# Mixture-of-experts tiles in the order of the routing batches, with the final sum and norm of finished batches placed inside the tile loop

## The chip, the cores and the metric

The program runs on one core of a Trainium2 chip. The metric is device time in microseconds (us) of one execution. Times below are medians of several executions, or rows of one profiled execution. The engines are TensorE (PE), VectorE (DVE), ScalarE (ACT), GpSimd (POOL) and SyncE (SP), which here only issues DMA transfers.

## The reference

16 sequences of 256 tokens, 256 channels, float32. A causal self-attention and a cross-attention (16 heads of 16 channels), each with a residual and a layer norm, give 4096 rows `x2`. They are followed by a mixture of 8 experts, of which every row takes 2:

```
logits = x2 @ router_w.T
topk_logits, topk_idx = top_k(logits, 2)
probs = softmax(topk_logits)
hmid = gelu(x2 @ w1[e].T + b1[e])        # 256 -> 512
y    = hmid @ w2[e].T + b2[e]            # 512 -> 256
out  = layernorm(x2 + sum over the 2 experts of prob * y)
```

## The kernel before

**Routing.** The attention part works through 32 blocks. In the second half of them each sequence's 256 rows are finished and routed in nine batches (`BATCHES`: seven of 4 x 128 tokens, two of 2 x 128). For each of its two experts a row gets the next free place in that expert's region of `xs_dram`, and POOL scatters the row there with its id and its two weights. `carry` holds, per expert, the next free place. After the last batch DVE turns the counts into a table (`tbli`, `aside`; L1428 to L1465): for each of 71 tiles of 128 gathered rows its expert and the place where it starts. Tiles stand by expert, all tiles of expert 0 first. Tiles past the last one are filled with rows that nobody reads.

**The tile loop** (`for j in range(TILES)`, 71 tiles). SP loads the tile's rows (`rows`, L477, 5 buffers) and the first-layer weights of its expert two tiles further on (`load_first(j + 2)`, L464, 512 KB, 4 buffers). Before it issues the weights of a tile it waits for `h_pe`, the first layer of the tile four places earlier. PE transposes the rows (L813), does the first layer (L824), transposes the next tile's rows, and then does the second layer of the tile before (L835). DVE adds the first bias (`add_first_bias`, L1473), ACT transposes out (L1034) and does the gelu (L1041), DVE adds the second bias, weighs, adds the residual and computes the row ids (`finish_tile`, L1483 to L1489), and POOL scatters the result into `p_dram` (L1636, 3 buffers `stored`). Each engine has one queue of instructions in program order, and SP's are in the order of its loop.

**The end.** When all 71 tiles are stored, SP loads the two halves of every token's sum from `p_dram` in six groups (`NORM_GROUPS`, L487), DVE adds them and takes mean and variance (`measure`, L1508 to L1517), ACT and DVE make the inverse root (L1055, L1057, L1525 to L1534), ACT normalises (L1063), and SP stores the rows (L492).

Of the kernel before, what the change touches and what calls it, by code (L numbers as in the profile page):

```python
# [10 lines left out]
I32 = mybir.dt.int32  # L11
# [27 lines left out]
NORM_GROUPS = (4, 4, 8, 8, 4, 4)  # L39
# [18 lines left out]
ROUTED = NT * max(BATCHES.values())  # L58

# [65 lines left out]
def decoder_block(nc, x, xT, ctxT, wqk_self, wv_self, wo_self, wq_x, wk_x, wv_x, wo_x, bo_self, bo_x,  # L125
# [4 lines left out]
    with ExitStack() as ctx:  # L130
# [82 lines left out]
        carry = sb("carry", [P, NE])  # L213
# [8 lines left out]
        cnt = sb("cnt", [P, 8, NE])  # L222
        cnti = sb("cnti", [P, 2, NE], I32)
        tbl = sb("tbl", [P, 2, TILES])
        tbli = sb("tbli", [P, 2, TILES], I32)
        aside = sb("aside", [P, TILES])
        surplus = sb("surplus", [P, TILES])
        jrows = sb("jrows", [P, TILES])
# [14 lines left out]
        def halves(group):  # L243

            n = NORM_GROUPS[group]
            at = sum(NORM_GROUPS[:group])
            flat = big[:] if at < 16 else w2s[:].rearrange("p c e f -> p (c e f)")
            k0 = (at % 16) * TOPK * E
            assert at % 16 + n <= 16
            return flat[:, k0:k0 + TOPK * n * E].rearrange("p (k n e) -> p k n e", k=TOPK, n=n)  # L250


# [47 lines left out]
        table_link, table_ready = sem("table_link"), sem("table_ready")  # L300
        pads_out = sem("pads_out")
# [17 lines left out]
        jrow = small[:, 32:32 + TILES]  # L319
        tri8 = small[:, 128:192].rearrange("p (e f) -> p e f", e=NE)  # L320
        assert 32 + TILES <= 128
# [50 lines left out]
        def stored_in(o):  # L372

            return len(range(o, TILES, OUT_BUFFERS))

        def expert_of(eng, j):
            return eng.value_load(tbli[0:1, 0, j:j + 1], min_val=0, max_val=NE - 1)

# [7 lines left out]
        def _(sp):  # L386
# [85 lines left out]

            for j in range(TILES):
                start = sp.value_load(tbli[0:1, 1, j:j + 1], min_val=0, max_val=PADS + NE * P - P)
                if j >= ROW_BUFFERS:
                    sp.wait_ge(rowid_ready, j - ROW_BUFFERS + 1)
                sp.dma_start(rows[:, j % ROW_BUFFERS, :], xs_dram[bass.ds(start, P), :]  # L477
                             ).then_inc(rows_in[j % ROW_BUFFERS], 16)
                load_first(j + 2)

            for o in range(OUT_BUFFERS):
                sp.wait_ge(stored[o], 16 * stored_in(o))
            for group, n in enumerate(NORM_GROUPS):
                r0 = P * sum(NORM_GROUPS[:group])
                src = p_dram[0:TOPK * N, :].rearrange("(k n) e -> k n e", k=TOPK)[:, r0:r0 + n * P, :]
                for k in range(TOPK):
                    sp.dma_start(halves(group)[:, k], src[k].rearrange("(p n) e -> p n e", p=P)  # L487
                                 ).then_inc(halves_in[group], 16)
            for group, n in enumerate(NORM_GROUPS):
                r0 = P * sum(NORM_GROUPS[:group])  # L490
                sp.wait_ge(normed, group + 1)
                sp.dma_start(out[r0:r0 + n * P, :].rearrange("(p n) e -> p n e", p=P), halves(group)[:, 1]  # L492
                             ).then_inc(out_done, 16)
            sp.wait_ge(out_done, 16 * len(NORM_GROUPS))

        @block.tensor
        def _(pe):
# [301 lines left out]

            pe.wait_ge(table_ready, 2)  # L800
# [48 lines left out]
        def _(act):  # L849
# [192 lines left out]

            turn_out(0)
            for j in range(TILES):
                if j + 1 < TILES:
                    turn_out(j + 1)
                gelu(j)

            def seed_group(group):
                if group >= len(NORM_GROUPS):  # L1050
                    return
                n = NORM_GROUPS[group]
                act.wait_ge(moments_ready, group + 1)
                yy, t0 = ls[:, group % 2, 1, 0:n], ls[:, group % 2, 2, 0:n]
                act.activation(t0, moments[:, group % 2, 0:n, 1], ACT.Ln, bias=eps[:, 1:2]).then_inc(tail_log, 1)  # L1055
                act.wait_ge(tail_log, group + 1)
                act.activation(yy, t0, ACT.Exp, scale=-0.5).then_inc(tail_seeded, 1)  # L1057

            def normalise_group(group):
                act.wait_ge(norm_ready, group + 1)  # L1060
                d = halves(group)
                for i in range(NORM_GROUPS[group]):
                    ins = act.activation(d[:, 1, i], d[:, 0, i], ACT.Identity, bias=ls[:, group % 2, 4, i:i + 1],  # L1063
                                         scale=ls[:, group % 2, 1, i:i + 1])
                ins.then_inc(normed, 1)

            act.preload_act_table_set("natural_log_exp_and_others")
            seed_group(0)
            for group in range(len(NORM_GROUPS)):
                seed_group(group + 1)  # L1070
                normalise_group(group)

        @block.vector
        def _(dve):
# [32 lines left out]
            def prepare_tables():  # L1107
                dve.tensor_scalar(rev[:], iota8, -1.0, float(NE), ALU.mult, ALU.add)
                dve.tensor_copy(carry[:], iota8_region)
                dve.tensor_scalar(jrows[:], jrow, float(P), None, ALU.mult)  # L1110
                dve.tensor_scalar(surplus[:], jrow, float(P), float(P * (1 - TOPK * N // P)), ALU.mult, ALU.add)
                dve.tensor_scalar(tokid[:], jrow[:, 0:N // P], float(P), pcol, ALU.mult, ALU.add
# [242 lines left out]
            def take_ranks(n):  # L1355
                if n is None:
# [4 lines left out]
                o = ring_slot(job).rearrange("p (j e) -> p j e", e=NE)  # L1361
                dve.tensor_tensor(rank[:, 0:nt, :], o[:, 0:nt, :],
                                  carry[:].unsqueeze(1).to_broadcast([P, nt, NE]), ALU.add).then_inc(router_link, 1)
                dve.wait_ge(router_link, next(n_route))
                dve.tensor_tensor(carry[:], o[:, nt, :], carry[:], ALU.add).then_inc(drained_by(job), 1)
# [16 lines left out]
            for q in range(QUARTERS):  # L1382
# [45 lines left out]
            dve.tensor_tensor(cnt[:, 1], carry[:], iota8_region, ALU.subtract).then_inc(table_link, 1)  # L1428
            dve.wait_ge(table_link, next(n_table))
            dve.tensor_scalar(cnti[:, 1], cnt[:, 1], float(P - 1), None, ALU.add).then_inc(table_link, 1)  # L1430
            dve.wait_ge(table_link, next(n_table))
            dve.tensor_scalar(cnti[:, 1], cnti[:, 1], 7, None, ALU.logical_shift_right
                              ).then_inc(table_link, 1)
            dve.wait_ge(table_link, next(n_table))
            dve.tensor_copy(cnt[:, 2], cnti[:, 1]).then_inc(table_link, 1)
            dve.wait_ge(table_link, next(n_table))
            w88 = sq[:].rearrange("p t e -> p (t e)")[:, 0:NE * NE].rearrange("p (a b) -> p a b", a=NE)
            dve.tensor_tensor(w88, tri8, cnt[:, 2].unsqueeze(1).to_broadcast([P, NE, NE]), ALU.mult
                              ).then_inc(table_link, 1)
            dve.wait_ge(table_link, next(n_table))  # L1440
            dve.tensor_reduce(cnt[:, 3], w88, AX.X, ALU.add).then_inc(table_link, 1)
            dve.wait_ge(table_link, next(n_table))
            dve.tensor_scalar(cnt[:, 4], cnt[:, 2], -float(P), float(REGION), ALU.mult, ALU.add
                              ).then_inc(table_link, 1)
            wj = [a.rearrange("p t e -> p (t e)")[:, 0:TILES * NE].rearrange("p (j e) -> p j e", e=NE)
                  for a in (sq[:], qkn[:, 0])]

            def every_j(ap):
                return ap.unsqueeze(1).to_broadcast([P, TILES, NE])

# [262 lines left out]
```

## Time and profile before

| | |
|---|---|
| median of 3 runs | 1171.24 us (1169.45 to 1173.36) |
| time of the profiled execution | 1169.33 us |
| its span, first to last instruction | 1167.6 us |
| PE busy | 1029.7 us, 88% |
| DVE busy | 724.1 us, 62% |
| ACT busy | 596.7 us, 51% |
| POOL busy | 267.0 us, 23% |
| mean DMA rate | 119 GB/s over the span |

The busy share is an average over three stages. The attention part runs to about 804 us, the routing of the last rows and the table to 850 us, the tile loop to 1120 us, and the end to 1167.6 us. In the tile loop PE is busy nearly all the time, in the end not at all. What a change is worth is read from the stage in which it lies.

### The profile page before, as it was taken

How to read it: one execution, taken by the hardware profiler on the slowest of the kernel's cores; microseconds unless marked ns; L12 is line 12 of the kernel's file. 1: busy time of each engine (PE TensorE's matmuls, PEld its weight loads, DVE VectorE, ACT ScalarE, POOL GpSimd, SP SyncE). 2: the span in 40 equal slices, each digit the busy share in tenths (PEclk: the TensorE clock that was granted, in tenths of full speed). 3: DMA queues.
4: the chain of work that ended last, by engine and by line, in shares of the span. 5: the costliest groups of instructions: out<-in, count | busy, mean ns of one | idle time of the engine just before them, and what ended most of it. 6: DMA issues, size and time to landing. Idle time of an engine off the chain costs nothing.

```text
span 1167.6 us, 29067 instructions
## 1 busy us (share of the span) xinstructions
PE 1029.7 (88%) x10925; PEld 767.3 (66%) x10925; DVE 724.1 (62%) x1584; ACT 596.7 (51%) x1024; POOL 267.0 (23%) x309
## 2 busy tenths in 40 slices
PE   6899999999999999999999999877189999999930
PEld 3556666666666666666666666545179999999930
DVE  4656666666677877677878787753524444444446
ACT  3567767767755566665555655654122222222225
POOL 1053232232232200000212121132512222222210
PEclk9999999999999999999999999998589999999975
DMA  7117446446441000100101100011267777677656
GB/s 290 29 36 249 149 144 209 147 146 211 142 126 30 12 20 12 47 12 20 40 26 35 34 26 30 13 40 40 92 203 215 219 215 210 213 214 218 202 201 253
DMA packets 95078, 139.25 MB, mean 119 GB/s; under 512 B 11264, under 2 KB 68992, under 8 KB 93920
## 3 DMA queue, kind: packets, MB, share of 16 engines
q1 hardware_dynamic: 88320, 114.98, 31.6%
q0 software_dynamic: 6624, 22.42, 4.9%
q8 instruction: 91, 1.49, 0.5%
q14 instruction: 43, 0.35, 0.1%
HBM read 76.56 MB, written 60.29 MB: 117 GB/s over the span
## 4 chain that ended last, share of the span: by engine, by line
PE 80%; issue 6%; DVE 5%; ACT 3%; DMA 2%; SPq 2%; another core or an unknown queue 0%; ACTq 0%; DVEq 0%; POOLq 0%
PE PS L824 11%; PE PS L561 11%; PE PS L835 11%; PE PS L582 10%; PE PS L531 5%; PE PS L635 5%; PE PS L639 5%; PE PS L706 5%; PE PS L653 4%; PE PS L680 3%; PE PS L538 2%; PE PS L669 2%; PE PS L534 2%; ACT pT L904 2%; PE PS L813 1%
## 5 line engine op out<-in xcount | busy, mean ns | idle before, releaser
L1158 DVE TENSOR_REDUCE part<-PS 128x6 f32<-128x768 f32 (+1 forms) x256 | 270.1, 1087 | 117.9 <-PE PS L538 85.0
L904 ACT ACTIVATE pT<-PS 128x768 f32<-128x768 f32 (+1 forms) x256 | 220.8, 915 | 102.6 <-PE PS L561 89.8
L561 PE MATMUL PS<-big 32*128 32x256 f32 (+1 forms) x2048 | 133.2, 373 | 20.4 <-issue 11.7
L1595 POOL TENSOR_SCALAR_AFFINE_SELECT pT<-pT 128x512 f32<-128x512 f32 x128 | 84.2, 659 | 278.7 <-ACT pT L904 274.9
L824 PEld LDWEIGHTS PS<-oT,big 128*128 128x128 f32 x1136 | 139.8, 194 | 5.4 <-ACT oT L1034 1.8
L824 PE MATMUL PS<-oT,big 128*128 128x128 f32 x1136 | 140.6, 278 | 1.0 <-ACT oT L1034 1.0
L561 PEld LDWEIGHTS PS<-big 32*128 32x128 f32 x2048 | 95.9, 184 | 62.5 <-issue 61.2
L582 PE MATMUL PS<-pT,vaug 128*32 128x256 f32 (+1 forms) x2048 | 125.0, 361 | 13.6 <-DVE sq L1227 3.5
L835 PE MATMUL PS<-w2s,qkn 128*128 x568 | 134.5, 380 | 0.0
L1034 ACT ACTIVATE oT<-PS 128x256 f32<-128x256 f32 x71 | 27.2, 383 | 192.7 <-PE PS L813 192.7
L1615 POOL DMA_INDIRECT xs_dram<-rows_all,posi x64 | 62.1, 971 | 250.1 <-PE PS L531 174.2
L1636 POOL DMA_INDIRECT p_dram<-pT,rowid x71 | 68.4, 964 | 212.6 <-DVE rowid L1489 208.4
L835 PEld LDWEIGHTS PS<-w2s,qkn 128*128 128x128 f32 x568 | 102.4, 190 | 11.5 <-issue 0.5
L915 ACT ACTIVATE oT<-PS 128x256 f32<-128x256 f32 x128 | 49.0, 383 | 113.5 <-PE PS L582 111.6
L582 PEld LDWEIGHTS PS<-pT,vaug 128*32 128x32 f32 x2048 | 58.8, 109 | 64.7 <-issue 39.5
L1473 DVE TENSOR_TENSOR qkn<-PS,b1T 128x512 f32<-128x512 f32 x71 | 49.1, 692 | 61.0 <-PE PS L824 61.0
L1483 DVE TENSOR_TENSOR pT<-PS,w_self 128x256 f32<-128x256 f32 x71 | 30.2, 425 | 88.5 <-PE PS L835 88.5
L531 PE MATMUL PS<-big 32*128 32x256 f32 x1024 | 74.2, 404 | 7.0 <-ACT pT L904 6.8
L639 PE MATMUL PS<-w_self,xin 128*128 128x512 f32 x128 | 66.9, 649 | 1.3 <-DVE w_self L1085 1.3
L531 PEld LDWEIGHTS PS<-big 32*128 32x128 f32 x1024 | 47.4, 186 | 20.8 <-issue 18.9
L1041 ACT ACTIVATE qkn<-qkn 128x512 f32<-128x512 f32 x71 | 44.7, 630 | 19.8 <-DVE qkn L1473 18.9
L1268 DVE TENSOR_TENSOR y<-PS,xb 128x512 f32<-128x512 f32 x32 | 22.1, 692 | 40.9 <-PE PS L706 37.3
(170 smaller groups left out, 1533.8 us busy)
## 6 DMA issues: line engine op xcount, KB each, us to landing
big<-w SPq DMA_DIRECT2D x71, 512.0 KB
xs_dram<-zrow SPq DMA_DIRECT2D x24, 1496.0 KB, 9.8
oT<-xs_dram SPq DMA_DIRECT2D x71, 136.0 KB
xin<-xT SPq DMA_DIRECT2D x16, 256.0 KB, 2.9
w2s<-w POOLq DMA_DIRECT2D x1, 4096.0 KB, 15.8
xb<-x SPq DMA_DIRECT2D x16, 256.0 KB, 11.2
xin<-ctxT SPq DMA_DIRECT2D x16, 256.0 KB, 2.8
big<-nmaxT SPq DMA_DIRECT2D x128, 4.0 KB
```

Of the source, the lines that this page charges most:

```text
L531: ins = pe.matmul(o, q, a[r0:r1, 1, g, :], start=True, stop=True)
L561: ins = pe.matmul(o, keys, a[r0:r1, 0, g, q0:T], start=True, stop=True)
L582: ins = pe.matmul(o[PADDED * i:PADDED * (i + 1), q0:T], vaug[:, n % 4, kt, head(g, i), :], pT[:, k % 2, i, kt * T:kt * T + T - q0], start= ...
L635: ins = pe.matmul(o[:, e0:e0 + E], a1[:, c, t * P:(t + 1) * P], w[:, c, :], start=(c == 0), stop=(c == KC - 1))
L639: ins = pe.matmul(o, a[:, c, t * P:(t + 1) * P], w_qk[:, c, :], start=(c == 0), stop=(c == KC - 1))
L824: ins = pe.matmul(moe_bank(1, j % 2)[:, f * P:(f + 1) * P], w1s[:, j % W1_BUFFERS, c, f * P:(f + 1) * P], xsT[:, j % 2, c * P:(c + 1) * P] ...
L835: ins = pe.matmul(moe_bank(3, j % 2)[:, 0:E], hact[:, j % 2, c * P:(c + 1) * P], w, start=(c == 0), stop=(c == FC - 1))
L904: act.activation(pT[:, k % 2, 2 * half:2 * half + 2, 0:wide], src, ACT.Exp).then_inc((exp_a, exp_b)[half], 1)
L1158: dve.tensor_reduce(dst, src, AX.X, ALU.max, negate=True).then_inc((max_a, max_b)[half], 1)
L1595: pool.affine_select(d, d, [[0, 2], [0, 2], [1, P]], ALU.is_ge, 0.0, base=0, channel_multiplier=-1).then_inc(masked, 1)
L1615: pool.indirect_dma_start(out=xs_dram, out_offset=bass.IndirectOffsetOnAxis(ap=posi[:, batch_index(last), c:c + 1], axis=0), in_=rows_all[ ...
L1636: pool.indirect_dma_start(out=p_dram, out_offset=bass.IndirectOffsetOnAxis(ap=rowid[:, o, 0:1], axis=0), in_=ye[:, o], in_offset=None).the ...
```

## The change

1. The routing counts are kept after each batch (`carries`, 10 rows instead of one `carry`), and the table orders tiles by the batch in which they begin, and by expert within a batch. After `DONE_BY[g]` tiles every row of the batches up to g has been computed: 15, 23, 31, 39, 47, 55, 63, 67 and 71 tiles.
2. The table is worked out on the partitions, one tile in each, turned by three PE transposes, and copied out of PSUM.
3. The final groups are the nine batches: seven of 4 x 128 tokens, two of 2 x 128. For a group g SP loads the halves in its loop step `DONE_BY[g] + 6`, DVE adds a quarter of them in each of its steps `DONE_BY[g] + 4` to `+ 7` and measures them, DVE works the roots out in steps `+ 8` to `+ 11` (by shift and subtraction and three Newton steps, without ACT), ACT normalises in steps `+ 13` and `+ 14`, and SP stores in its step `+ 21`. Groups 6, 7 and 8 (`ENDING`) take their roots after the loop in the old way.
4. The loaded halves lie in `big` behind the weight buffers, in `vaug` and in `rows_all`.

```diff
+NORM_GROUPS = tuple(NT * k for _, k in sorted(BATCHES.items()))
+DONE_BY = tuple((TOPK * P * sum(NORM_GROUPS[:g + 1]) - P) // P + NE for g in range(CLASSES))
+FETCH, MEASURE, ROOTS, NORMALISE, SEND = 6, 4, 8, 13, 21
+ENDING = tuple(g for g in range(CLASSES) if DONE_BY[g] + ROOTS + 4 > TILES)
...
+        def group_step(j, at):
+            for g in range(CLASSES):
+                if g not in ENDING[1:] and 0 <= j - DONE_BY[g] - at < 4:
+                    return g, j - DONE_BY[g] - at
+            return None
...
+            def fetch_group(group):
+                for o in range(OUT_BUFFERS):
+                    sp.wait_ge(stored[o], 16 * stored_by(DONE_BY[group], o))
+                n, r0 = NORM_GROUPS[group], P * sum(NORM_GROUPS[:group])
+                src = p_dram[0:TOPK * N, :].rearrange("(k n) e -> k n e", k=TOPK)[:, r0:r0 + n * P, :]
+                for k in range(TOPK):
+                    sp.dma_start(halves(group)[:, k], src[k].rearrange("(p n) e -> p n e", p=P)
+                                 ).then_inc(halves_in[group], 16)
...
                 load_first(j + 2)
-
-            for o in range(OUT_BUFFERS):
-                sp.wait_ge(stored[o], 16 * stored_in(o))
-            for group, n in enumerate(NORM_GROUPS):
...
+                if j - FETCH in DONE_BY:
+                    fetch_group(DONE_BY.index(j - FETCH))
+                if j - SEND in DONE_BY:
+                    send_group(DONE_BY.index(j - SEND))
+
+            for group in range(CLASSES):
+                if DONE_BY[group] + FETCH < TILES:
+                    continue
+                if group == CLASSES - 1:
+                    send_group(ENDING[0] - 1)
+                fetch_group(group)
+            for group in ENDING:
+                send_group(group)
...
                 gelu(j)
+                place = group_step(j, NORMALISE)
+                if place is not None and place[1] < 2:
+                    group, step = place
+                    act.wait_ge(norm_ready, group + 1)
+                    for i in range(2):
+                        normalise_rows(group, 2 * step + i)
...
+            def add_halves(group, i):
+                if i == 0:
+                    dve.wait_ge(halves_in[group], 32)
+                d = halves(group)
+                dve.tensor_tensor(d[:, 0, i], d[:, 0, i], d[:, 1, i], ALU.add).then_inc(added, 1)
...
             for j in range(1, TILES):
                 before, e = e, expert_of(dve, j)
                 add_first_bias(j, e)
+                add_halves_at(j)
                 finish_tile(j - 1, before)
+                measure_at(j)
             finish_tile(TILES - 1, e)
```

SP's queue in the tile loop, one step of it before: `tbli` is read for the tile's place, the rows are loaded, `tbli` is read for the expert, and the weights (`big<-w`) go out behind the wait for `h_pe`.

```order
L474 TENSOR_LOAD tbli
L474 ISA x2
L477 ISA [waits rowid_ready]
L477 DMA oT<-xs_dram 128x272
L461 TENSOR_LOAD tbli
L461 ISA x2
L464 ISA [waits h_pe]
L464 DMA big<-w 128x2x512
```

The same step of the changed kernel where a group is fetched (group 3, whose halves lie in `vaug`):

```order
L523 ISA [waits rowid_ready]
L523 DMA oT<-xs_dram 128x272
L492 TENSOR_LOAD tbli
L492 ISA x2
L495 ISA [waits h_pe]
L495 DMA big<-w 128x2x512
L510 DMA vaug<-p_dram 128x1024 [waits stored_2,stored_1,stored_0]
L510 DMA vaug<-p_dram 128x1024
```

The two loads of 512 KB stand behind the weight load of the same step, and so behind its wait for `h_pe`.

DVE's queue in the tile loop, one tile before: first bias of tile j, then the finishing of tile j - 1.

```order
L377 TENSOR_LOAD tbli
L377 ISA x2
L1473 ISA [waits hact_ready,h_pe]
L1473 TENSOR_TENSOR qkn<-PS,b1T 128x512
L1483 ISA [waits stored_0,y_pe]
L1483 TENSOR_TENSOR pT<-PS,w_self 128x256
L1487 ISA [waits biased]
L1487 SCALAR_TENSOR_TENSOR pT<-pT,oT 128x256
L1489 ISA
L1489 TENSOR_TENSOR rowid<-oT,aside 128x1
```

The same of the changed kernel in the first of a group's measuring steps (group 0, j = 19), up to the next tile's first bias:

```order
L1544 ISA [waits hact_ready,h_pe]
L1544 TENSOR_TENSOR qkn<-PS,b1T 128x512
L1569 TENSOR_TENSOR big<-big 128x256 [waits halves_in_0]
L1554 ISA [waits stored_0,y_pe]
L1554 TENSOR_TENSOR pT<-PS,w_self 128x256
L1558 ISA [waits biased]
L1558 SCALAR_TENSOR_TENSOR pT<-pT,oT 128x256
L1560 ISA
L1560 TENSOR_TENSOR rowid<-oT,aside 128x1
L1573 BN_STATS stats<-big 128x6 [waits added]
L397 TENSOR_LOAD tbli
L397 ISA x2
```

A sum of halves that waits for `halves_in_0` now stands between the first bias of tile j and the finishing of tile j - 1, and a statistics instruction before the next tile's expert is read.

## Rows read from the trace of the kernel before

**Rows 1.** Windows, tile loop: us, busy per engine, PEclk, DMA share, GB/s
```profile
850.00:1100.00 250.00, 248.67 (x1715) 234.27 (x1716) 108.66 (x259) 68.50 (x134) 61.69 (x64) 0.99 0.70 212
```

**Rows 2.** Chain that ended last, one tile: start us, us, what
```profile
1082.75 0.22 PE PS L813 x2
1082.97 1.73 PE PS L835 x8
1084.70 1.78 PE PS L824 x16
```

**Rows 3.** Timeline, one tile: start us, us, engine, line, tiles [idle before]
```profile
1053.04 0.69 DVE L1473 TENSOR_TENSOR qkn<-PS,b1T 128x512 f32<-128x512 f32 x1 [0.66 <-PE PS L824]
1053.07 0.56 SPq L464 DMA_DIRECT2D big<-w  x1
...
1053.77 0.63 ACT L1041 ACTIVATE qkn<-qkn 128x512 f32<-128x512 f32 x1 [0.23 <-DVE qkn L1473]
...
1054.99 0.42 DVE L1483 TENSOR_TENSOR pT<-PS,w_self 128x256 f32<-128x256 f32 x1 [1.26 <-PE PS L835]
...
1055.96 0.15 DVE L1489 TENSOR_TENSOR rowid<-oT,aside 128x1 int32<-128x1 f32 x1
```

**Rows 4.** Timeline, start of the tile loop, weight loads and first bias
```profile
843.50 2.06 SPq L464 DMA_DIRECT2D big<-w  x2
...
847.53 0.55 SPq L464 DMA_DIRECT2D big<-w  x1
...
850.00 0.56 SPq L464 DMA_DIRECT2D big<-w  x1
...
855.48 0.55 SPq L464 DMA_DIRECT2D big<-w  x1
855.52 0.69 DVE L1473 TENSOR_TENSOR qkn<-PS,b1T 128x512 f32<-128x512 f32 x1 [13.12 <-PE PS L824]
```

**Rows 5.** Timeline, the end: last second layer to last norm
```profile
1117.68 2.28 PE L835 MATMUL PS<-w2s,qkn 128*128 x9
...
1124.49 3.18 SPq L487 DMA_DIRECT2D big<-p_dram  x6
...
1129.34 1.22 DVE L1508 TENSOR_TENSOR big<-big 128x1024 f32<-128x1024 f32 x1 [8.10 <-DMA big<-p_dram]
...
1132.04 0.38 DVE L1517 BATCH_NORM_AGGREGATE moments<-stats 128x2 f32<-128x6 f32 x4
...
1159.11 0.38 DVE L1517 BATCH_NORM_AGGREGATE moments<-stats 128x2 f32<-128x6 f32 x4 [1.60 <-ACT w2s L1063]
...
1160.16 4.04 ACT L1063 ACTIVATE w2s<-w2s,ls 128x256 f32<-128x256 f32 x8
...
1160.67 0.16 DVE L1534 SCALAR_TENSOR_TENSOR ls<-moments,ls 128x4 f32<-128x4 f32 x1
```

**Rows 6.** DMA issues, 1124.3 to 1124.8 us: count, KB each, us to landing
```profile
big<-p_dram SPq DMA_DIRECT2D x1, 512.0 KB, 3.6
```

**Rows 7.** Timeline of DVE and PE around the table
```profile
836.24 0.16 DVE L1428 TENSOR_TENSOR cnt<-carry,small 128x8 f32<-128x8 f32 x1
...
839.11 0.74 DVE L1453 TENSOR_TENSOR sq<-cnt,small 128x568 f32<-128x568 f32 x1
...
842.17 0.23 DVE L1465 TENSOR_TENSOR tbli<-tbl,jrows 128x71 int32<-128x71 f32 x1
...
850.32 0.66 PE L813 MATMUL PS<-ident,oT 128*128 128x128 f32 x2 [18.14 <-DMA oT<-xs_dram]
```

**Rows 8.** Timeline of PE, two places with an idle gap
```profile
737.42 2.06 PE L531 MATMUL PS<-big 32*128 32x256 f32 x16 [2.29 <-ACT pT L904]
739.41 1.79 PE L582 MATMUL PS<-pT,vaug 128*32 128x256 f32 x16
...
804.39 1.07 PE L582 MATMUL PS<-pT,vaug 128*32 128x256 f32 x16 [1.79 <-ACT pT L904]
```

**Rows 9.** Windows behind those gaps; columns as in Rows 1
```profile
737.00:741.00 4.00, 3.58 (x32) 1.96 (x32) 2.63 (x6) 1.68 (x3) 0.59 (x1) 0.57 0.02 4
805.00:809.00 4.00, 3.88 (x27) 2.82 (x16) 0.86 (x3) 0.77 (x3) 3.08 (x4) 0.60 0.35 125
```

More of the change, by code:

```diff
@@ L245, in halves @@
             n = NORM_GROUPS[group]
[L246 to L249, printed above, removed]
+            if group < 2:
+                flat, first = big[:, W1_BUFFERS * KC * F:], 0
+            elif group < 4:
+                flat, first = vaug[:].rearrange("p n t h d -> p (n t h d)"), 2
+            else:
+                flat, first = rows_all[:].rearrange("p t e -> p (t e)"), 4
+            k0 = TOPK * E * sum(NORM_GROUPS[first:group])
             return flat[:, k0:k0 + TOPK * n * E].rearrange("p (k n e) -> p k n e", k=TOPK, n=n)
+        wide = pflat[:, 0:3 * P].rearrange("p (a t) -> p a t", a=3)
         cst = pflat[:, 0:3 * P].rearrange("p (a t) -> p a t", a=3)
@@ L318, in decoder_block @@
         idcol = small[:, 17:18]
[L319 removed]
+        jrow = small[:, 32:32 + N // P]
         tri8 = small[:, 128:192].rearrange("p (e f) -> p e f", e=NE)
[L321 removed]
         def bc(ap, n):
@@ L479, in _ @@
                 load_first(j + 2)
-            for o in range(OUT_BUFFERS):
-                sp.wait_ge(stored[o], 16 * stored_in(o))
-            for group, n in enumerate(NORM_GROUPS):
[L484 to L494, printed above, removed]
+                if j - FETCH in DONE_BY:
[10 more added lines that the diff above has]
+                send_group(group)
+            sp.wait_ge(out_done, 16 * CLASSES)
         @block.tensor
@@ L798, in _ @@
                     fold_bias()
+            pe.wait_ge(columns_ready, 3)
+            for i in range(3):
+                ins = pe.transpose(bank(0)[:, i * P:(i + 1) * P], wide[:, i, :], ident[:])
+            ins.then_inc(table_pe, 1)
             pe.wait_ge(table_ready, 2)
@@ L1434, in _ @@
[L1434 to L1449, printed above, removed]
-            dve.tensor_tensor(wj[0], every_j(cnt[:, 3]), bc(jrow, NE), ALU.is_le).then_inc(table_link, 1)
@@ new lines, in _ @@
+            linked(dve.tensor_tensor(grown[:], grown[:], ends[:], ALU.subtract))
+            dve.tensor_scalar(offset[:, CLASSES * NE:], ends[:, CLASSES - 1, NE - 1:NE], -float(P), float(PADS),
+                              ALU.mult, ALU.add)
+            linked(dve.tensor_tensor(grown[:], grown[:], begun[:, 0:CLASSES], ALU.add))
+            linked(dve.scalar_tensor_tensor(out=o8, in0=grown[:], scalar=float(P), in1=of_batches(iota8_region),
+                                            op0=ALU.mult, op1=ALU.add))
@@ new lines, in sum_up @@
+            def sum_up(group):
+                n = NORM_GROUPS[group]
+                for i in range(n):
+                    dve.wait_ge(norm_link, next(n_norm))
+                if group >= 2:
+                    dve.wait_ge(normed, group - 1)
+                for i in range(n):
+                    ins = dve.bn_aggr(moments[:, group % 2, i, :], stats[:, 4 * (group % 2) + i, :])
+                if group in ENDING:
+                    ins.then_inc(moments_ready, 1)
+                else:
+                    ins.then_inc(norm_link, 1)
+                    dve.wait_ge(norm_link, next(n_norm))
```

203 lines of the change are left out of this document (132 added, 71 removed).

## The prediction

> **What bounds the kernel now.** I read the page first: PE is busy 88% of the span, so the question is where the other 12% lie. The windows by stage answer it. In the tile loop PE is busy 248.67 of 250 us, DVE 108.66, ACT 68.50, and the DMA engines 70% at 212 GB/s [rows 1]: PE is the bound, and everything else is cover. The chain that ended last shows what one tile costs there: 0.22 us of transposes, 1.73 of the second layer, 1.78 of the first, in all 3.73 us, with nothing in between [rows 2]. In the end stage PE does nothing. It stops at 1117.68 + 2.28 = 1119.96, call it E, and the span ends at 1167.6. So 47.6 us of the program lie behind E, with loads, sums and norms in a chain [rows 5]. This is what the change can win. What it can lose lies in the two other places it touches: the table before the loop, where PE waits, and the loop, where any microsecond in which PE stands still is lost whole.
>
> **The end stage, cost by cost.** Now: the last tile is stored and the first load of halves is issued 4.5 us behind E (1124.49). Then come 4096 tokens, until the last norm at 1160.16 + 4.04 = 1164.20, and 3.4 us more to the end for the last store [rows 5]. After: the same 4.5 us stand, since the last group must wait for the last tile. The last group has 256 tokens: two loads of 256 KB. One of 512 KB landed in 3.6 us [rows 6], and I add 0.4 for the second issue: they are there at E + 8.5. For four rows of tokens per partition DVE took from 1129.34 to 1132.04 + 0.38 = 1132.42, 3.1 us; two rows take half, and links a little: 1.7, E + 10.2. From the end of the last aggregate (1159.49) to the end of its last root step (1160.83) are 1.35 us. Two rows of norm at 4.04 / 8 = 0.505 are 1.0. With 3.4 for the last store the end is at E + 16.0. Groups 6 and 7 lie under the wait for the last tile: they are three times the work of group 8, some 5 us of DVE and 3 of ACT by the same rates, and start at E or before. The end stage falls from 47.6 to 16.0: **31.6 us won**. Bounds: 29, if groups 6 and 7 reach into group 8, and 33.
>
> **The table.** Now 14 DVE instructions run from 836.24 to 842.40, 6.2 us, four of them of 0.74 us [rows 7]. The other ten so take 0.32 each with their gaps. After: 23 instructions before the transposes, two of the big kind: 21 x 0.32 + 2 x 0.74 = 8.2. Then three PE transposes of 128x128, of which two took 0.66 there (PE's clock is low in that stage) [rows 7]: 1.0. Three copies out of PSUM, less than the 0.42 of one twice as wide [rows 3]: 0.9 in all. Two hops between engines: 0.3. Together 10.4, so **4.2 us lost**. Nothing covers it: SP's first weight load goes out behind the table, at 843.50 [rows 4]. Bounds: 2.5 (small instructions at 0.22) and 5.5.
>
> **The loop: DVE's and ACT's added work is covered.** A tile in which DVE sums and measures a quarter of a group adds 1.22 / 4 = 0.3 and about 0.35 us. A root step adds three or four linked operations of 0.16 to 0.2, the first of them four aggregates (0.38) as well [rows 5]: 0.6 to 1.1. DVE finishes a tile at 1055.96 + 0.15, 3.1 us behind its start at 1053.04 [rows 3]. It then comes up to 1.3 us late to the next bias. That bias and the gelu take 1.36 us (1053.04 to 1054.40), and PE wants them only 0.22 + 3.73 = 3.95 us behind the first layer. So 2.6 us are spare: nothing lost. Two norms on ACT, 1.0 us in two tiles of a group, go the same way.
>
> **The loop: DVE's wait for the halves is not covered.** Here I followed who waits for whom. At the start of the loop SP issues two weight loads, then two more, and the fifth at 855.48, beside the first bias of the first tile at 855.52 [rows 4]. The same pair stands in each tile, 1053.07 and 1053.04 [rows 3]. So SP's load of weights i + 4 goes out when the first layer of tile i ends, in SP's loop step i + 2. The change fetches a group in SP's step `DONE_BY + 6`, behind that load. This is the end of the first layer of tile `DONE_BY + 4`. And `DONE_BY + 4` is the tile behind whose bias DVE waits for the same halves. Both are released by one event, T. DVE must therefore wait out the whole landing, and the finishing of a tile, the reading of an expert and the next bias are queued behind it.
>
> How long: the fetch is issued at about T + 0.8, behind 0.56 us of weight issue. Two loads of 512 KB took 1129.34 - 1124.49 = 4.85 us with no traffic before them [rows 5], which gives T + 5.7. The 512 KB of weights are ahead of them. At 212 / 0.70 = 303 GB/s [rows 1] these alone move for 1.7 us, in part while the fetch starts up. I take T + 7.0. With the tile's rows and its store ahead as well (776 KB, 2.6 us) it is T + 8.3. Behind the landing: sum 0.3, finishing 1.1 (1054.99 to 1056.11), statistics 0.35, the expert's number at most the 0.66 us that DVE idles now, I take 0.5, bias and gelu 1.36 [rows 3], hops 0.2: 3.8. PE gets tile i + 1 at T + 10.8. It wanted it at T + 0.22 + 2 x 3.73 = T + 7.7. **PE stands still for 3.1 us** (1.3 at the early landing with the shortest chain, 4.6 at the late one), in groups 0 to 5. For group 6 SP's last steps have no weights left to wait for, so its fetch goes out some 2 us before T, and 2.6 us of slack take the rest.
>
> The Trainium skill, "DMA: Bandwidth & Descriptors", section "Anatomy of one DMA", fits a load as 2.0 us plus bytes at 436 GB/s. For the two loads that is 4.4 us, where this trace has 4.85, and the measurement decides; the page speaks of loads issued by GpSimd. With the weights ahead it would be T + 5.7, a stall of 1.8 us and an estimated total of 1162 us.
>
> **The clock behind a gap.** In the trace PE's granted clock falls from its upper level (2.4 GHz) to the lower (1.2) behind short gaps too. Behind a gap of 2.29 us the next four microseconds have a mean of 0.57, and behind one of 1.79 us 0.60 [rows 8, 9]. In the first case L582 takes 1.79 us, and 1.07 where the clock is high. Over that and L531 (2.06, by the same ratio 1.23) the loss is 0.72 + 0.83 = 1.5 us [rows 8]. The tile loop's matmuls are denser than those, so that a gap may be borne better there. Ends: nothing, and 3.0 for two such stretches. I take 1.5.
>
> **The sum.** Six groups at 3.1 + 1.5 = 4.6 are 27.6 us lost. 1169.33 - 31.6 + 4.2 + 27.6 = 1169.5 for an execution like the profiled one. This lies 1.9 us below the median of 1171.24, so the median to expect is between 1169.5 and 1171.4: **1171 us**. Two large terms cancel; the point where the loop's loss eats the gain is (31.6 - 4.2) / 6 = 4.57 us per group.
>
> **Rivals.**
> - *The wait is there, but PE keeps its upper clock.* For it speaks the dense loop, against it [rows 9]. 1169.33 - 31.6 + 4.2 + 6 x 3.1 = **1160.5**. Chance 0.17.
> - *The halves land early,* at T + 5.7: a stall of about 1.8 us, and 1.5 for the clock: 6 x 3.3 = 19.8, **1161.7**. For it speaks that a single load landed in 3.6 us and the second only 1.3 us later [rows 5, 6], so these move faster than the weights; against it, that the weights are issued first on the same queue. Chance 0.12. The fit of the Trainium skill named above would give this one.
> - *The kernel becomes slower: the landing is late.* With send, weights, rows and store ahead the halves land at T + 8.3 or later, PE stands still for 4.6 us, and the gap is long enough that the clock stays low for two stretches: 7.6 x 6 = 45.6, **1187.5**. It decides from 4.57 us per group. For it speaks that in four of six groups a store of 512 KB goes out one step before the fetch; against it, that this store has a whole tile to drain. Chance 0.15.
> - *There is no wait worth the name,* because SP runs further ahead than [rows 4] say. Then only the end and the table count: **1142**. The two rows beside each other speak against it. Chance 0.06.
>
> **How the numbers follow.** My own case has a chance of 0.50 and a range of 1163 to 1180. 0.3% (3.5 us) is about what a measurement of this kernel can tell from no change. Within my case I give 0.16 below 1167.7, 0.20 between, 0.14 above 1174.8. Faster: 0.16 + 0.17 + 0.12 + 0.06 = 0.51. Same: 0.20. Slower: 0.14 + 0.15 = 0.29. The range of 1153 to 1185 leaves out the case without a wait and the later half of the slower one.
>
> **What would show it.** In the profile after: DVE's sum of halves with six waits of about 6 us for the load, each followed by an idle gap of PE of some 3 us before a second layer and a window of clock 0.5; a distance from PE's last matmul to the span's end of 16 us; a first transpose of the tile loop about 4 us later than 850.32; all other tiles at 3.73 us. Wrong would make it: waits of DVE shorter than 3.5 us, a gap without a fall of the clock, or tiles that take longer than 3.73 us where no group is fetched.

## The result and the profile after

The changed kernel takes **1187.97 us** (median of 4 runs, 1186.28 to 1190.98), the kernel before beside it 1170.37 (4 runs, 1169.45 to 1173.36). The ratio is 1.0149, 95% interval 1.0119 to 1.0178: 17.6 us slower. I had forecast 1171, so almost no change, with a range of 1153 to 1185, a chance of 0.51 for faster and of 0.29 for slower. The time is outside the range, and on the side that I held less likely than faster.

The profiled execution took 1189.02 us. The page's first lines, to be held against a span of 1167.6 us and a PE that was busy 88% of it:

```profile
span 1187.3 us, 29198 instructions
...
PE 1051.2 (89%) x10928; PEld 780.8 (66%) x10928; DVE 735.8 (62%) x1687; ACT 594.2 (50%) x1018; POOL 267.7 (23%) x309
```

PE issues the same matmuls, but for the three transposes of the table (10928 against 10925), and is busy for 21.5 us more. That alone doesn't tell whether it works or works slowly. The windows do. First the whole tile loop, from the first transpose to PE's last matmul, then two stretches of it (us, busy time of PE, PEld, DVE, ACT, POOL, granted clock, DMA share, GB/s):

```profile
857.85:1172.78 314.93, 285.96 (x1846) 263.36 (x1846) 148.66 (x439) 85.47 (x168) 66.78 (x69) 0.94 0.63 210
...
947.00:949.00 2.00, 2.00 (x11) 2.00 (x11) 1.32 (x4) 0.00 (x0) 0.00 (x0) 0.50 0.30 109
...
1090.00:1092.00 2.00, 0.00 (x0) 0.00 (x0) 1.86 (x6) 0.66 (x2) 0.97 (x1) 0.50 0.25 66
```

The same window of the kernel before, for the same stretch of its program:

```profile
850.32:1119.96 269.64, 268.63 (x1846) 252.36 (x1846) 117.77 (x281) 74.46 (x144) 66.50 (x69) 0.99 0.68 204
```

The loop is 45.3 us longer with the same 1846 records of PE. Of these, 28.0 are idle time of PE (314.93 - 285.96, less the 1.0 of before), and 285.96 - 268.63 = 17.3 are longer busy time. Most of that is the clock: it has a mean of 0.94 in place of 0.99, and in the second row it is 0.50, the lower level of 1.2 GHz, while PE is busy all the time. Taken in windows of 1 us, busy time times the missing share of the clock adds up to 14.0 us in the seven places where the clock falls (an estimate from these windows). In the loop before, the clock is below its upper level only in the first 7 us. The other 3.3 us are at full clock. PE's records overlap where it runs without a break: transposes last 0.38 us and the next matmul begins 0.22 behind them. Beside a gap they stand alone and count whole; that this is the 3.3 us is an argument, but a run below has 3.3 us more busy time too, with gaps and no fall of the clock. The waits of the loop say for whom (us in total, times, longest):

```profile
DVE rows_all L1569 <- DMA rows_all<-p_dram: 21.0, 3, 8.9
PE PS L862 <- DMA oT<-xs_dram: 19.3, 9, 9.2
PE PS L884 <- DVE pT L1554: 17.0, 7, 2.6
DVE vaug L1569 <- DMA vaug<-p_dram: 14.1, 2, 7.1
DVE big L1569 <- DMA big<-p_dram: 13.2, 2, 7.2
```

Seven waits of DVE for halves, 48.3 us together; seven waits of PE for DVE's finishing of a tile, 17.0 us; and nine of PE for the rows of a tile, of which the longest, 9.2, is the first transpose's before the loop. The other eight hold 10.1 us. The timeline of group 0 shows how they hang together:

```profile
933.13 0.69 DVE L1544 TENSOR_TENSOR qkn<-PS,b1T 128x512 f32<-128x512 f32 x1 [0.66 <-PE PS L873]
933.16 0.56 SPq L495 DMA_DIRECT2D big<-w  x1
933.84 1.00 SPq L510 DMA_DIRECT2D big<-p_dram  x2
...
935.93 0.35 SPq L523 DMA_DIRECT2D oT<-xs_dram  x1
...
941.01 0.42 DVE L1569 TENSOR_TENSOR big<-big 128x256 f32<-128x256 f32 x1 [7.19 <-DMA big<-p_dram]
...
941.36 0.42 DVE L1554 TENSOR_TENSOR pT<-PS,w_self 128x256 f32<-128x256 f32 x1
941.36 0.44 PE L862 MATMUL PS<-ident,oT 128*128 128x128 f32 x2 [0.92 <-DMA oT<-xs_dram]
...
942.92 0.69 DVE L1544 TENSOR_TENSOR qkn<-PS,b1T 128x512 f32<-128x512 f32 x1
...
944.41 2.49 PE L884 MATMUL PS<-w2s,qkn 128*128 x8 [2.60 <-DVE pT L1554]
946.69 3.14 PE L873 MATMUL PS<-oT,big 128*128 128x128 f32 x16
```

Read it as a chain. DVE's bias and SP's weight load begin 0.03 us apart, so one event T (933.13) releases both. The fetch goes out at T + 0.71, and DVE stands at its sum until T + 7.88. The finishing, the next bias and the gelu follow, and PE gets its second layer at T + 11.28 after two gaps, 0.92 and 2.60 us. The eight matmuls of second layer then take 2.49 us and the sixteen of first layer 3.14, where the same rows of an undisturbed tile have 1.89 and 1.95 (936.77 and 934.77; the 1.73 and 1.78 of [rows 2] are from start to start): the price of the clock. The rows of a tile, issued behind the megabyte of halves on SP's queue (935.93), are the 0.92, and DVE's late finishing is the 2.60.

The end stage, which answers to [rows 5]:

```profile
1168.99 3.79 PE L884 MATMUL PS<-w2s,qkn 128*128 x16
...
1177.33 0.79 SPq L510 DMA_DIRECT2D rows_all<-p_dram  x2
...
1180.62 0.76 DVE L1569 TENSOR_TENSOR rows_all<-rows_all 128x256 f32<-128x256 f32 x2 [3.29 <-DMA rows_all<-p_dram]
...
1183.77 1.09 ACT L1094 ACTIVATE rows_all<-rows_all,ls 128x256 f32<-128x256 f32 x2 [0.82 <-DVE ls L1657]
```

PE ends at 1168.99 + 3.79 = 1172.78, and 14.5 us of program follow where there were 47.6.

The table, which answers to [rows 7]:

```profile
840.34 0.23 DVE L1497 TENSOR_TENSOR ends<-carries,small 128x72 f32<-128x72 f32 x1
...
847.72 0.90 PE L847 MATMUL PS<-ident,pT 128*128 128x128 f32 x3 [11.29 <-DVE pT L1529]
...
857.85 0.66 PE L862 MATMUL PS<-ident,oT 128*128 128x128 f32 x2 [9.23 <-DMA oT<-xs_dram]
```

From its first instruction to the first transpose of the loop it takes 17.5 us, before 14.1 (836.24 to 850.32). So the two profiles differ by -33.1 (end) + 3.4 (table) + 45.3 (loop) = 15.6 us, and the table begins 4.1 us later, which makes the 19.7 of the spans. Most of those 4.1 can't be laid to the change: 3.4 of them are already there where PE begins its first block (30.46 against 27.02), and in the runs below, whose code up to there is that of the change, this point lies anywhere between 26.7 and 30.5.

### The profile page after: what moved, and what is told of

Read it like the earlier page. It is cut to its first block and busy times, and to the rows that moved or that the text cites. A ratio compares the mean times of both kernels' runs of the same rounds, so it can differ in the third digit from the quotient of the medians.

```text
span 1187.3 us, 29198 instructions
## 1 busy us (share of the span) xinstructions
PE 1051.2 (89%) x10928; PEld 780.8 (66%) x10928; DVE 735.8 (62%) x1687; ACT 594.2 (50%) x1018; POOL 267.7 (23%) x309
## 5 line engine op out<-in xcount | busy, mean ns | idle before, releaser
L884 PE MATMUL PS<-w2s,qkn 128*128 x568 | 144.4, 400 | 17.9 <-DVE pT L1554 17.0
L873 PEld LDWEIGHTS PS<-oT,big 128*128 128x128 f32 x1136 | 145.0, 200 | 6.2 <-ACT oT L1083 1.8
L873 PE MATMUL PS<-oT,big 128*128 128x128 f32 x1136 | 144.7, 283 | 1.0 <-ACT oT L1083 1.0
L884 PEld LDWEIGHTS PS<-w2s,qkn 128*128 128x128 f32 x568 | 107.4, 199 | 33.3 <-issue 20.6
```

Of the source, the lines that this page charges most:

```text
L873: ins = pe.matmul(moe_bank(1, j % 2)[:, f * P:(f + 1) * P], w1s[:, j % W1_BUFFERS, c, f * P:(f + 1) * P], xsT[:, j % 2, c * P:(c + 1) * P] ...
L884: ins = pe.matmul(moe_bank(3, j % 2)[:, 0:E], hact[:, j % 2, c * P:(c + 1) * P], w, start=(c == 0), stop=(c == FC - 1))
```

## The experiments

All ratios below are against the kernel before, run on the same chip beside them. Apart from the change itself they come in three sets, each on a chip of its own: the table alone and the fetch at 4, 5 and 7; then the next four; then the last three. The kernel before had a median of 1171.4, 1171.89 and 1164.39 us in them, so ratios are compared and not times. The loop runs from the first transposes behind the table to PE's last matmul.

| kernel | median us | ratio (95%) | loop | of it PE busy | end |
|---|---|---|---|---|---|
| the change | 1187.97 | 1.0149 (1.0119, 1.0178) | 314.9 | 286.0 | 14.5 |
| table alone | 1176.07 | 1.0038 (1.0021, 1.0054) | 269.7 | 268.6 | 48.1 |
| fetch at 4 | 1159.87 | 0.9899 (0.9868, 0.9929) | 286.7 | 274.4 | 14.6 |
| fetch at 5 | 1182.8 | 1.0085 (1.0053, 1.0117) | 310.9 | 284.2 | 14.6 |
| fetch at 7 | 1204.24 | 1.0271 (1.0232, 1.0309) | 334.4 | 286.9 | 14.5 |
| DVE two tiles later | 1173.02 | 1.0010 (0.9993, 1.0027) | 297.5 | 279.7 | 14.7 |
| fetch ahead of weights | 1170.79 | 0.9992 (0.9966, 1.0019) | 297.6 | 280.4 | 14.6 |
| fetch in quarters | 1149.5 | 0.9817 (0.9785, 0.9848) | 276.6 | 272.0 | 14.6 |
| fetch on ACT's queue | 1152.15 | 0.9824 (0.9786, 0.9861) | 283.1 | 275.4 | 14.6 |
| fetch at 4, rows ahead | 1132.91 | 0.9720 (0.9693, 0.9747) | 270.0 | 268.9 | 14.5 |
| the change, rows ahead | 1178.59 | 1.0109 (1.0075, 1.0144) | 320.7 | 286.4 | 14.5 |
| quarters, rows ahead | 1130.32 | 0.9712 (0.9687, 0.9737) | 268.5 | 267.5 | 14.6 |

Loop, busy and end are of one profiled execution each.

### When the fetch goes out: step 4, 5 or 7

The theory said that only the place of the fetch in SP's loop makes DVE wait. One number changes:

```diff
-FETCH, MEASURE, ROOTS, NORMALISE, SEND = 6, 4, 8, 13, 21
+FETCH, MEASURE, ROOTS, NORMALISE, SEND = 4, 4, 8, 13, 21
```

and 5 or 7 in the two others.

> The change with one number different: a group's halves are fetched two loop steps of SP earlier (FETCH = 4 in place of 6), everything else as in the change. Theory (DVE waits for halves that are asked for by the same event that releases it): the halves lie there when DVE comes, no gap of PE, no fall of its clock, and the loop goes back from 315 us to about 270. About 1143 us, so some 45 below the change and 27 below before. Rival (the added DMA traffic or DVE's added work stretches the loop by itself): the loop stays above 300 us and the time above 1175.

> As the change, fetched one step later (FETCH = 7). Theory: each of the seven groups in the loop waits one tile period more, 7 x 3.73 = 26 us: 1210 to 1218 us. Rival (traffic or added work): no different from the change, 1188.

> As the change, fetched one step earlier (FETCH = 5). Theory: the landing moves 3.73 us towards DVE, from 7 to 9 us behind the event down to 3.4 to 5.2. PE had 3.9 us of slack less the chain of 3.4, so only the groups that land late keep a gap of under 1 us: 1143 to 1150 us. Rival (traffic or added work): above 1175, as with two steps.

At 7 the kernel is slower than before by 2.7%, and the seven gaps of PE before the second layer add up to 45.0 us, where the change has 17.0. The direction is the one that the wait gives, the size is smaller: 1204 and not 1210 to 1218, since DVE's waits grew by 2.3 us a group and not by a tile's 3.73 (64.7 in all, against 48.3). At 4 the kernel gets faster than before, though not the 1143 us of the theory: the loop is 28.2 us shorter than in the change, and no gap of PE is put down to DVE any more. So the wait of DVE is a cause. But at 4 some 17 us of the loop's loss stayed, and at 5 nearly all of it, although the DVE waits were down to 2.9 to 5.1 us. There PE's idle gaps add up to 25.7 us, and 23.9 of them stand before transposes. My expectation for 5 was wrong by over 30 us. The timeline of fetch at 5 shows what took the place of the wait:

```profile
994.57 1.81 SPq L510 DMA_DIRECT2D vaug<-p_dram  x2
996.43 0.42 SPq L516 DMA_DIRECT2D result<-big  x1
...
997.61 0.35 SPq L523 DMA_DIRECT2D oT<-xs_dram  x1
...
1005.91 0.69 PE L862 MATMUL PS<-ident,oT 128*128 128x128 f32 x2 [4.73 <-DMA oT<-xs_dram]
```

The rows of a tile (136 KB) are issued at 997.61 and PE gets them 8.3 us later: a megabyte of halves and 512 KB of output were issued on SP's queue just ahead. In this run the send of group g and the fetch of group g + 2 fall in one SP step (21 = 16 + 5). The five groups with both gave gaps of 3.8 to 5.0 us, and the two first, which have no send beside them, 0.4 and 1.6. So most of what the fetch at 5 costs goes with the burst of both together, and the step of the fetch changes two things: how early the halves are asked for, and how far they are from a send. No run moved the send alone. With the fetch at 4, where the send comes a step later, a gap before transposes that is put down to the rows is 1.20 us at most:

```profile
964.51 0.44 PE L862 MATMUL PS<-ident,oT 128*128 128x128 f32 x2 [1.20 <-DMA oT<-xs_dram]
```

Of its 11.4 us of added gaps the profile puts 4.0 down to the rows; 7.3 have no releaser (1.5 before the transposes of group 0, 5.8 before second layers). That these too hang on when the rows are issued is shown further down, where the rows go out earlier and all of these gaps go.

### The table by itself

The new table and its transposes, with the old loop and the old end stage.

> The new order of the tiles and the new table on DVE and PE, with the old tile loop and the old end stage (all 4096 tokens summed and normed after the last tile). Theory: costs only the longer table, 3 to 4 us: 1173 to 1175 us. Rival (the order of the tiles by batch makes the tile loop slower, or the start of the program is 3.4 us later because of the added setup): 1177 or more, the loop longer than 270 us or the first block later.

```profile
858.62:1128.27 269.65, 268.64 (x1846) 252.61 (x1846) 117.70 (x281) 74.45 (x144) 66.49 (x69) 0.99 0.66 204
```

The loop is 269.65 us long, before 269.64. The order of tiles costs nothing, the table 4.5 us (0.38%; 3 to 4 were expected, and 4.2 in the prediction).

### Halves as late as before, DVE two tiles later

This leaves the fetch where the change has it and takes the wait away from the other side:

```diff
-FETCH, MEASURE, ROOTS, NORMALISE, SEND = 6, 4, 8, 13, 21
+FETCH, MEASURE, ROOTS, NORMALISE, SEND = 6, 6, 10, 14, 22
...
-                if g not in ENDING[1:] and 0 <= j - DONE_BY[g] - at < 4:
+                if g not in ENDING and 0 <= j - DONE_BY[g] - at < 4:
...
-            sum_up(ENDING[0])
+            measure(ENDING[0])
```

> The fetch stays where the change has it (SP's step DONE_BY + 6), but DVE sums and measures two tiles later (MEASURE 6, ROOTS 10, NORMALISE 14, SEND 22; group 6 is measured behind the loop). First theory, of two costs of a fetch: DVE's wait for the halves is gone here, and what is left is that the tile's rows stand behind 1 MB on SP's queue: gaps of PE of 0.5 to 1.5 us before a transpose, loop 280 to 290 us, total 1157 to 1165 us, like the run with the fetch two steps earlier. Rival (DVE's wait is all there is): no gaps, about 1147 us. Rival (traffic itself slows the loop): above 1180.

There is no DVE wait for halves left in the loop. It is still 27.9 us longer than before, with 16.8 us of gaps, 14.8 of them before transposes:

```profile
1068.42 1.04 SPq L510 DMA_DIRECT2D rows_all<-p_dram  x2
1069.52 0.42 SPq L516 DMA_DIRECT2D result<-vaug  x1
...
1070.73 0.31 SPq L523 DMA_DIRECT2D oT<-xs_dram  x1
...
1079.33 0.69 PE L862 MATMUL PS<-ident,oT 128*128 128x128 f32 x2 [4.29 <-DMA oT<-xs_dram]
```

That is the second cost without the first, but not at the size that it has in the change: this edit moves the send into the fetch's step as well (22 = 16 + 6). The two groups without a send have gaps of 0.16 and 0.60 us, the next four with one 2.60 to 4.29 (the last, with a single tile left to load, 0.50), and with them 1173 us came out and not 1157 to 1165. The clock falls behind these gaps too: of the 11.1 us by which PE's busy time is longer, 9.1 are at the lower level (from the 1 us windows, as above).

### Fetch and send ahead of the weight load

If the weights ahead of the halves were what delays them, issuing the halves first should help.

```diff
+                if j - FETCH in DONE_BY:
+                    fetch_group(DONE_BY.index(j - FETCH))
+                if j - SEND in DONE_BY:
+                    send_group(DONE_BY.index(j - SEND))
                 load_first(j + 2)
-                if j - FETCH in DONE_BY:
-                    fetch_group(DONE_BY.index(j - FETCH))
-                if j - SEND in DONE_BY:
-                    send_group(DONE_BY.index(j - SEND))
```

(with `FETCH` at 4).

> As the run with FETCH = 4, but fetch and send are issued ahead of the step's weight load and not behind it, so about one microsecond or more earlier, and the next tile's rows have one megabyte less directly before them. If the remaining gaps of PE (0.3 to 1.5 us before a transpose, seven times) come from rows that queue behind the fetch: they shrink to under 0.5 us, total 1147 to 1155 us. Rival (the gaps come from the total traffic of the DMA engines in these tiles): unchanged, 1157 to 1163.

It moved the wrong way, against both expectations: slower than fetch at 4 by 0.9%. Group 1 of this run:

```profile
954.44 0.38 PE L862 MATMUL PS<-ident,oT 128*128 128x128 f32 x2
...
955.70 0.81 SPq L510 DMA_DIRECT2D big<-p_dram  x2
957.33 0.56 SPq L495 DMA_DIRECT2D big<-w  x1
958.67 0.36 SPq L523 DMA_DIRECT2D oT<-xs_dram  x1
...
964.27 0.44 PE L862 MATMUL PS<-ident,oT 128*128 128x128 f32 x2 [2.21 <-DMA oT<-xs_dram]
```

and of the run with the fetch at 4, up to the gap shown above (964.51):

```profile
955.68 0.38 PE L862 MATMUL PS<-ident,oT 128*128 128x128 f32 x2
...
956.02 0.56 SPq L495 DMA_DIRECT2D big<-w  x1
956.76 0.93 SPq L510 DMA_DIRECT2D big<-p_dram  x2
958.77 0.35 SPq L523 DMA_DIRECT2D oT<-xs_dram  x1
```

The same bytes stand ahead of the next rows in both, and the rows take the same time from issue to use, 5.6 and 5.7 us. But they are issued 4.2 us behind the transposes of the step here and 3.1 there: with the halves first, the weights go out 2.55 us later and the rows 1.1 us later. The gap is longer by 1.0 us. Over the loop seven such gaps of 1.2 to 2.6 us make 13.5. So putting the halves first makes what stands behind them late, and it is the next rows that PE misses.

### Smaller pieces, another queue, rows a step earlier

Three edits that take the rows out from behind the burst in different ways, all with the fetch at 4 or its like. In quarters, one for each of four SP steps:

```diff
+            def fetch_quarter(group, i):
...
+                    sp.dma_start(halves(group)[:, k, i], src[k].rearrange("(p n) e -> p n e", p=P)[:, i]
+                                 ).then_inc(quarter_in[i], 16)
```

(the store in quarters too). On ACT's queue, ACT issues both, the fetch at its iteration `DONE_BY + 2`:

```diff
+                        act.dma_start(halves(group)[:, k], src[k].rearrange("(p n) e -> p n e", p=P)
+                                      ).then_inc(halves_in[group], 16)
```

And SP issues each tile's rows one step earlier:

```diff
+            load_rows(0)
             for j in range(TILES):
+                load_rows(j + 1)
                 load_first(j + 2)
```

> The fetch of a group is cut in four pieces of 256 KB, one per loop step from DONE_BY + 4 on, each waited for by the sum of that quarter alone, and the send in four pieces of 128 KB from DONE_BY + 17 on. The same bytes, never more than 256 KB ahead of a tile's rows. Theory (rows behind a burst in SP's queue): no gaps, loop at 270 us, total 1143 to 1148 us. Rival (total traffic, or smaller descriptors of 1 KB, cost as much): 1157 or more.

> Whole groups again, but fetch and send are issued by ACT on its own queue, at the time at which the run with FETCH = 4 issues them on SP's. If it is the order within SP's queue that delays the rows: the two queues share the DMA engines packet by packet, the rows are delayed less, total 1145 to 1153 us. Rival (the DMA engines are simply busy with the megabyte): as with FETCH = 4, 1157 to 1163.

> FETCH = 4 with whole bursts of 1 MB on SP's queue, and every tile's rows loaded one loop step earlier than in the change (step j loads the rows of tile j + 1). Theory (rows lack the lead to stand behind a burst): the lead grows from 1.6 periods to 2.6, no gap before a transpose is left, total 1145 to 1150 us. Rival (the DMA engines cannot carry the bursts beside the tiles): 1157 or more, as with FETCH = 4 alone.

All three are faster than fetch at 4 (ratios 0.9817, 0.9824 and 0.9720 against 0.9899). The quarters leave 3.7 us of gaps, only 0.7 of it before a transpose, and are the run with 3.3 us more busy time and no fall of the clock behind the first 7 us. The run on ACT's queue came out as expected, the quarters 1.5 us above the expected 1143 to 1148, and the rows a step earlier below their 1145 to 1150, of which some 7 us are the faster set. Of the three, only the rows a step earlier bring the loop back whole. Quarters first, then rows ahead:

```profile
855.72:1132.34 276.62, 271.96 (x1846) 252.58 (x1846) 149.37 (x439) 86.17 (x168) 67.02 (x69) 0.99 0.79 239
...
848.25:1118.29 270.04, 268.94 (x1846) 252.62 (x1846) 149.03 (x439) 86.33 (x168) 66.80 (x69) 0.99 0.76 245
```

The loop with rows ahead is 0.4 us longer than before, with 245 GB/s in place of 204 and DVE busy for 149 us in place of 118. So neither DVE's and ACT's added work nor the added traffic costs PE anything, once nothing waits for a transfer that is issued too late. On ACT's queue some of the loss stays (6.7 us of added gaps, 2.9 of them put down to the rows, and two DVE waits of 1.1 and 1.0 us), so the order on one queue isn't all of it; that rows issued with little time to spare also share the DMA engines with the burst is a likely reading that no run isolates.

The rival to this reading was that the rows alone are what makes the change slow. The same edit, made to the change with its fetch at 6:

> The change itself (FETCH = 6) with the rows loaded one step earlier. Theory of two costs: the rows' part goes and DVE's wait stays: DVE waits 6 to 9 us in each group, PE has one gap of 2.5 to 3.5 us before a second layer and none before a transpose, the clock falls behind it, loop 300 to 308 us, total 1176 to 1182 us. Rival (the two overlap so far that only DVE's wait counts): 1188, unchanged.

```profile
932.63 0.42 DVE L1575 TENSOR_TENSOR big<-big 128x256 f32<-128x256 f32 x1 [7.95 <-DMA big<-p_dram]
...
936.03 2.50 PE L890 MATMUL PS<-w2s,qkn 128*128 x5 [4.50 <-DVE pT L1560]
```

No gap before a transpose is left, and the seven before the second layer have grown from 17.0 to 33.3 us: the loop is not shorter at all. The two costs lie over each other, since in each group the late rows only take up time that PE would have spent waiting for DVE. The ratio is 1.0109 against 1.0149, and their intervals overlap, so these runs don't tell the two kernels apart. The median of 1178.59 lies in the expected 1176 to 1182, but for the wrong reason: the kernel before was some 7 us faster in this set, while the expected loop of 300 to 308 us measured 320.7. (The profile shown is the slowest execution of this kernel, 1186.24 us, so its loop is longer than the usual.)

### Both together

Quarters, and the rows a step earlier.

> The fetch and the send in quarters, and the rows one step earlier. Both theories of the loop's cost say that nothing is left: loop 269.6 to 272 us, and with the table 2.5 longer and the end at 14.6 us a total of 1141 to 1146 us, the shortest of all. Rival (the gaps that the quarters left are those of the traffic): 1149 as before.

1130.32 us beside 1164.39 for the kernel before, 0.9712 (0.9687 to 0.9737): faster than both kernels, and below the expected 1141 to 1146 by more than the 7 us of this set. Behind the first two tiles, which wait for ACT for 0.5 us each as in every run, the profile lists no idle gap of PE in its loop, and the loop of 268.5 us is no longer than before. Against rows ahead by itself (0.9720) the intervals overlap, so the quarters add nothing that these runs can tell.

## Why the prediction was wrong

**The end stage** was right in its path and nearly in size: 31.6 us won were predicted, with bounds of 29 to 33, and 33.1 measured. The last loads took 3.3 us and not 4.0, and the last store 2.4 and not 3.4. Groups 6 and 7 are done under the wait for the last tile, as said.

**The table** was right: 4.2 predicted, 3.4 in the profile and 4.5 in the timed runs of the table alone.

**DVE's and ACT's added work** was costed at nothing, and with the rows ahead it costs 0.4 us over the whole loop.

**The wait** of DVE was right as a mechanism: one event for fetch and sum, DVE held until the landing, PE behind it, the lower clock behind PE's gap. The waits of DVE were 6.0 to 8.9 us in groups 0 to 5. Asking for the halves two steps earlier gives 2.5% back.

**The step that failed is the loop's term**, "Six groups at 3.1 + 1.5 = 4.6 are 27.6 us lost". It measured 45.3 us, and all three of its factors were too small, seven groups at 4.0 + 2.0 + 0.5 in place of six at 3.1 + 1.5:

- *The gap:* 28.0 / 7 = 4.0 us a group, and not 3.1. In group 0 the landing came at T + 7.9 and not T + 7.0, the chain behind it took 3.4 us and not 3.8, and the gap was 3.5. The later groups, with a send one step ahead, waited up to 8.9 us. My bounds for the landing, T + 5.7 to T + 8.3, held it in group 0. The value I chose within them came from the weights' bytes at the loop's mean rate. The late rows of a tile, which end the first of the two gaps in groups 0 to 5, are in these 4.0 us too, but don't add to them: with the rows issued earlier the gaps are no smaller. The fit of the Trainium skill, "DMA: Bandwidth & Descriptors", section "Anatomy of one DMA", would have put the landing at T + 5.7, an estimate. This trace has 7.9 in group 0, so the measurement decides; the fit is for loads issued by GpSimd, and this one stands behind half a megabyte in a busy loop.
- *The clock:* 14.0 / 7 = 2.0 us a group, and not 1.5. I had priced one short stretch at the lower level; here it lasts about a whole tile or more. Another 3.3 / 7 = 0.5 us a group of busy time at full clock had no term in my sum.
- *The count:* seven groups, and not six. I had let group 6 off because SP has no weights left to wait for. Its fetch did go out 2.5 us before the bias, but DVE came late to that bias from group 5's root steps, the halves took 7.3 us to land, and DVE found them missing for 4.1 us more:

```profile
1152.96 1.71 SPq L510 DMA_DIRECT2D rows_all<-p_dram  x2
...
1155.47 0.69 DVE L1544 TENSOR_TENSOR qkn<-PS,b1T 128x512 f32<-128x512 f32 x1 [1.25 <-issue]
...
1160.30 0.43 DVE L1569 TENSOR_TENSOR rows_all<-rows_all 128x256 f32<-128x256 f32 x1 [4.14 <-DMA rows_all<-p_dram]
...
1163.71 3.31 PE L884 MATMUL PS<-w2s,qkn 128*128 x8 [1.93 <-DVE pT L1554]
```

With the measured sizes the sum is 1169.33 - 33.1 + 3.4 + 45.3 = 1184.9, and the 4.1 us by which the table began later make it the 1189.0 of the profile.

**The rival on the slower side** came nearest, with 0.15 of the chance: a landing at T + 8.3, 4.6 us of gap, two stretches of low clock, deciding from 4.57 us a group, 1187.5 us. The measured 6.5 us a group lie behind that point. That its time is within 0.5 us of the measured median is luck: six groups at 7.6 make about what seven at 6.5 do. What I held against it, that the store has a whole tile to drain, was not a row but an argument, and the waits speak for either side: 7.2 and 6.0 us in the two groups without a send, 7.1, 7.0, 8.9 and 8.0 in the four with one.

**What I didn't see** is that the tile's rows queue behind the same burst. I put the rows ahead of the halves in a sum of bytes, but didn't ask who waits for the rows behind them. In the change this is covered by DVE's wait: rows ahead changes its ratio by less than these runs can tell. Where the wait is gone it is the loss: all but 0.4 of the 17.1 us of loop with the fetch at 4, as rows ahead shows, and most of the 27.9 us with DVE two tiles later, where a send in the same step makes it larger.

**Still open:** in the run on ACT's queue the loop is 13.5 us longer than before, 6.7 of it idle and 6.8 busy time; the clock falls once there, behind gaps of 1.82 and 0.81 us, which is 3.1 us of the busy time. What PE waits for in 3.4 us of its gaps, and in the 7.3 of those with the fetch at 4 that have no releaser in the profile, is not shown. And why the wait at one and the same place is 6.0 us in one group and 8.9 in another is told only roughly by what was issued ahead of it.

## What to carry to other kernels

When a load is added to a queue, look in both directions: at who waits for it, and whether the event that releases it is the one that releases its consumer; and at the small loads behind it on the same queue, with the time that each had to spare. An issue two loop steps earlier for the consumer's load and one step earlier for the small one cost nothing here and was worth 4.2% of the time (1.0149 to 0.9720). One of the two alone was worth less: 2.5% for the first, nothing that can be told for the second. The groups of the fetch at 5 with and without a send suggest to keep two large transfers out of one step, too. Where PE is the bound, count a gap with what follows it: here 4.0 us of gap brought 2.5 more, 2.0 of it by the clock, and a sum in which two large terms cancel needs each factor of the larger one checked against its worst row.

## What the runs showed of the hardware

- Two loads of 512 KB take 4.85 us from issue to use with no load before them [rows 5]; behind 512 KB of weights on one queue, in a loop that moves 210 GB/s, they take 7.2 us in group 0 (933.84 to 941.01).
- A tile's rows (136 KB) issued behind a megabyte take 5.6 and 5.7 us until PE uses them (958.67 to 964.27 with the fetch ahead of the weights, 958.77 to 964.51 with the fetch at 4). With 512 KB of output ahead of them as well it is 8.3 and 8.6 us (997.61 to 1005.91, 1070.73 to 1079.33).
- In the change PE's clock fell while PE was busy without a break: behind the gaps of 0.92 and 2.60 us, the second ending at 944.41, it was 0.88 from 945 to 946 and 0.50 from 946 to 949, and a first layer took 3.14 us in place of 1.95. With the fetch at 4 it fell in one group only, behind gaps of 1.50 and 0.41 us (0.50 from 933 to 935); behind the other six groups' gaps of up to 1.38 us it stayed at its upper level.
- PE's busy time in the profile grows with gaps even at full clock: 271.96 against 268.63 us in quarters, for the same 1846 records.
- The time until PE's first block lay between 26.7 and 30.5 us in executions of code that is the same up to there, which is as much as the difference that a measurement can tell here. A stage's length is the safer number to compare than its place.
